# Top-k attention: the guess's last two steps on VectorE, and the softmax division moved from the attention to the projection

## The chip, the cores and the metric

The kernel runs on one core of one Trainium2 chip. The metric is device time in microseconds of one execution. Times are given as the median of several executions; the profile is one further execution taken by the hardware profiler.

## The reference

Two attention layers over x of shape [2, 256, 48, 48], so 2304 positions, 8 heads of 32, all in float32. The change touches only the first one:

```python
scores = einsum('bhnd,bhmd->bhnm', q, k) * DHEAD ** (-0.5)
kth = top_k(scores, 64)[0][..., -1:]
masked = where(scores >= kth, scores, finfo.min)
attn = softmax(masked, axis=-1)
o = einsum('bhnm,bhmd->bhnd', attn, v)      # then back to [B, C, H, W]
o = conv1x1(o, Wo, bo) + x                  # project_out
...                                         # two 1x1 convolutions with batch norms, then the second attention
```

Each row of scores keeps its 64 largest; the softmax runs over these.

## The kernel before

The stages follow one another, with a block of instructions per engine in each: `project_heads` (q, k, v), `attention_top`, `project_out`, `mlp`, then the second layer's projection, full attention and output.

`attention_top` works on tiles of 128 query rows against all 2304 keys, two tiles (u = 0 and 1) making a pair. There are 8 heads of 18 pairs, 144 pairs. Each engine has its instructions in an order written out by hand, and waits on semaphores for the others. For one pair:

- TensorE computes the scores of a tile (L363); ScalarE copies them out of PSUM (`keep_scores`, L446) into one of four buffers.
- VectorE takes the eight largest of each chunk of 36 scores, 64 instructions a tile (`chunk_tops`, L565), then `prepare` (L573 to L576). A tile's completion raises `tops_taken`.
- The 64th largest value is sought near a guess. `guess_place` makes the guess in four dependent ScalarE steps for each tile: a weighted sum of the chunks' first two values (L478, with an accumulator), a count of the candidates above it by Sign (L481, likewise), a linear `factor` from that count (L484), and the product of factor and sum (L487).
- `select` on VectorE waits for both guesses (L590), marks and counts the candidates above (L593), finds the next 24 below in three rounds (L598 to L609) and picks the right one (L613). L617 computes whether a row is in doubt. It runs after the first eight instructions of the next pair's `chunk_tops`.
- TensorE and ScalarE condense the doubts to one number (L390 to L392, L467). `hand_on` on VectorE reads it after twelve more of `chunk_tops`, counts again (L635) and if needed searches again (L648, L650) where there is doubt, and then signals `kth_ready` (L671).
- ScalarE writes a penalty (L462), GpSimd subtracts it from the scores (L547), ScalarE takes the exponentials with their sums in an accumulator (L450).
- TensorE transposes the probabilities (L373), ScalarE copies these out (L457), TensorE multiplies them with v into four quadrants (L382). ScalarE copies the quadrants (`parts`, L531), TensorE adds them (L401), and `finish` (L495) copies the two tiles' results out, each scaled by its row's 1/sum, which `invert_sums` (L676) made on VectorE.

ScalarE's order in one turn of the loop is: guess of tile 0 of the next pair, exponentials of tile 0, scores, guess of tile 1, two copies of transposed blocks, exponentials of tile 1, three copies, scores, the doubt, two copies, the wait for `kth_ready`, the two penalties with three copies between them, `parts`, `finish`.

`project_out` turns the results in 9 chunks of 512 positions (`turn`, L752), ScalarE copies them (L779), TensorE multiplies with the weights (L767), VectorE adds bias and x (L791). TensorE's order is turn(0), then for each chunk c: turn(c + 1), the eight matmuls of chunk c.

Of the kernel before, what the change touches and what calls it, by code (L numbers as in the profile page):

```python
# [19 lines left out]
F32 = mybir.dt.float32  # L20
# [251 lines left out]

def attention_top(nc, cst, operands, q_parts, k_parts, v_all, o_all):

    ctx = ExitStack()
    with ctx:
# [24 lines left out]
        above = sb("above", [P, 1])  # L301
        sums = sb("sums", [P, 2])
        one_by_sum = [sb(f"one_by_sum{n}", [P, 2]) for n in range(2)]
        parts = sb("parts", [P, PAIR])
# [8 lines left out]
        tops_taken, dve_order = sem("tops_taken"), sem("dve_order")  # L313
        guess_steps, guess_ready = sem("guess_steps"), sem("guess_ready")
        doubt_ready, doubt_counted, any_ready = sem("doubt_ready"), sem("doubt_counted"), sem("any_ready")
# [3 lines left out]
        weighed, parts_ready, added, o_kept = sem("weighed"), sem("parts_ready"), sem("added"), sem("o_kept")  # L319
        inverse_ready = sem("inverse_ready")  # L320
        HEAD_PAIRS = B * PAIRS
# [121 lines left out]
        def _(act):  # L443
# [3 lines left out]

            def exponentials(s, tile, parity):
                act.wait_ge(masked_ready, tile + 1)
                act.activation(probs[s % 2][:, :], probs[s % 2][:, :], ACT.Exp, scale=SCALE,  # L450
                               bias=minus_max[parity][:, s % 2:s % 2 + 1], accum_out=sums[:, s % 2:s % 2 + 1]
                               ).then_inc(probs_ready, 1)
# [17 lines left out]
            def guess_place(u, pair, parity):  # L470

                step = (2 * pair + u) * 3
                act.wait_ge(tops_taken, 2 * pair + u + 1)
                act.activation(weighted[:, u, :, :], top8[parity][:, u, 0:CHUNKS, 0:2], ACT.Identity,  # L478
                               scale=-FIRST_GUESS / CHUNKS, accum_out=minus_first[:, u:u + 1]).then_inc(guess_steps, 1)
                act.wait_ge(guess_steps, step + 1)  # L480
                act.activation(compared[:, u, :, :], top8[parity][:, u, 0:CHUNKS, 0:KEEP], ACT.Sign,  # L481
                               bias=minus_first[:, u:u + 1], accum_out=balance[:, u:u + 1]).then_inc(guess_steps, 1)
                act.wait_ge(guess_steps, step + 2)
                act.activation(factor[:, u:u + 1], balance[:, u:u + 1], ACT.Copy, scale=-STEP / 2,  # L484
                               bias=-(1.0 + STEP * (CHUNKS * KEEP / 2 - AIM))).then_inc(guess_steps, 1)
                act.wait_ge(guess_steps, step + 3)
                act.activation(guess[:, u:u + 1], factor[:, u:u + 1], ACT.Identity,  # L487
                               scale=minus_first[:, u:u + 1]).then_inc(guess_ready, 1)

            def finish(s, h, pair, parity):  # L490

                act.wait_ge(inverse_ready, pair + 1)
                act.wait_ge(added, pair + 1)
                for u in range(2):
                    last = act.activation(o_all[:, s + u, cols(h * D, D)], ps_o[:, O_COL + D * u:O_COL + D * u + D],  # L495
                                          ACT.Identity, scale=one_by_sum[parity][:, u:u + 1])
                last.then_inc(o_kept, 1)

# [6 lines left out]
            for u in range(2):  # L505
                penalty(u, 0)
            with act.Fori(0, HEADS) as h:
                for p in range(HEAD_PAIRS):
                    pair, tile, s, parity = h * HEAD_PAIRS + p, h * HEAD_TILES + 2 * p, 2 * p, p % 2
                    guess_place(0, pair + 1, 1 - parity)  # L510
                    exponentials(s, tile, parity)
                    keep_scores(s + 4, tile + 4)
                    guess_place(1, pair + 1, 1 - parity)
                    keep_turned(s, 0, tile)
                    keep_turned(s, 1, tile)
                    exponentials(s + 1, tile + 1, parity)
# [12 lines left out]
                    penalty(1, 1 - parity)  # L529
                    act.wait_ge(weighed, tile + MCH + 3)  # L530
                    act.activation(parts[:, :], ps_o[:, 0:PAIR], ACT.Copy).then_inc(parts_ready, 1)  # L531
                    finish(s, h, pair, parity)

# [17 lines left out]
        def _(dve):  # L551
# [27 lines left out]
            def select(pair, tops):  # L579
# [7 lines left out]
                below_of = lambda u: below[:, u, :].rearrange("p (c k) -> p c k", k=KEEP)  # L587
                marks_of = lambda u: scratch[:, 0:(CHUNKS + REST) * KEEP].rearrange("p (c k) -> p c k", k=KEEP)
                after(at["n"])
                wait_alone(dve, guess_ready, 2 * pair + 2)  # L590
                written = [0, 0]
# [81 lines left out]

            def invert_sums(tile, pair, parity):
                wait_alone(dve, probs_ready, tile + 2)
                dve.reciprocal(one_by_sum[parity][:, :], sums[:, :]).then_inc(inverse_ready, 1)  # L676

            dve.memset(flag[:, :], 0.0)
# [6 lines left out]

            def pair_step(pair, tile, p, before=2):

                def between(c):
                    if c == 7 and before > 0:
                        select(pair - 1, top8[(p - 1) % 2])  # L690
                    if c == 19 and before > 0:
                        hand_on(pair - 1, (p - 1) % 2)
                        if before > 1:
                            invert_sums(tile - 4, pair - 2, p % 2)

                chunk_tops(tile, 2 * p, between)
                chunk_tops(tile + 1, 2 * p + 1)
                prepare(pair, top8[p % 2])

            for p in range(2):  # L700
                pair_step(p, 2 * p, p, before=p)
            with dve.Fori(0, HEADS - 1) as h:
# [5 lines left out]
            dve.wait_ge(doubt_ready, ALL_PAIRS)  # L708
            dve.sem_inc(tops_taken, 2)
            invert_sums(HEADS * HEAD_TILES - 4, ALL_PAIRS - 2, 0)  # L710
            hand_on(ALL_PAIRS - 1, 1)
# [3 lines left out]
            dve.sem_inc(kth_ready, 1)  # L715
            invert_sums(HEADS * HEAD_TILES - 2, ALL_PAIRS - 1, 1)


def project_out(nc, cst, xs, o_all, x, w_o, b_o, mlp_weights, next_sources):

# [3 lines left out]
    with ctx:  # L724
        sb = lambda name, shape, dt=F32: ctx.enter_context(nc.sbuf_tensor("r_" + name, shape, dt))
        sem = lambda name: ctx.enter_context(nc.semaphore("r_" + name))
        w, bias = sb("w", [P, KC, C]), sb("bias", [P, KC])
        a = [sb(f"a{n}", [P, KC, CW]) for n in range(2)]
# [3 lines left out]
        turned, a_ready, proj_done, added = sem("turned"), sem("a_ready"), sem("proj_done"), sem("added")  # L732
        xf = xs[:, :, :, :].rearrange("p k b n -> p k (b n)")
        block = ctx.enter_context(nc.Block())
# [10 lines left out]
        def _(pe):  # L745
            def turn(c):
                for kc in range(KC):
                    n = KC * c + kc
# [32 lines left out]
        @block.vector  # L781
        def _(dve):
            dve.wait_ge(w_loaded, 32)
            for c in range(NCH):
                for piece in first_needed(c):
                    dve.wait_ge(x_loaded[piece], 16 * KC)
                for oc in range(KC):
# [3 lines left out]
                    dve.scalar_tensor_tensor(x_c, ps[n % 4][:, :], bias[:, oc:oc + 1], x_c,  # L791
                                             ALU.add, ALU.add).then_inc(added, 1)


# [515 lines left out]
def build(nc, t, out):  # L1310
# [4 lines left out]
    with ctx:  # L1315
# [4 lines left out]
        with ExitStack() as top:  # L1320
# [7 lines left out]
            o_top = top.enter_context(nc.sbuf_tensor("o_top", [P, B * MCH, C], F32))  # L1328
            attention_top(nc, cst, operands, q_parts, k_parts, v_top, o_top)
            project_out(nc, cst, xs, o_top, t["x"], t["w_o"], t["b_o"], mlp_weights, t)  # L1330
        mlp(nc, cst, xs, x1, mlp_weights, t["w_2"], (t["w_k1"], t["w_q1"], t["w_v1"]))
# [42 lines left out]
```

## Time and profile before

| | us |
|---|---|
| median of 3 executions | 5868.32 (5866.23 to 5868.85) |
| the profiled execution, its time | 5872.33 |
| the profiled execution, its span | 5870.2 |
| busy: TensorE, VectorE, ScalarE, GpSimd | 4366.5, 4365.0, 4327.3, 1500.0 |
| mean granted TensorE clock | 0.819 |

The span is from the first to the last instruction of the core. Busy times are of one profiled execution, and a busy TensorE is not a TensorE at its peak. In the rows, PE is TensorE, DVE VectorE, ACT ScalarE, POOL GpSimd, and L12 is line 12 of the kernel. "Idle before" is the time for which the engine had nothing to do just ahead of an instruction, with the releaser that ended it; "issue" there means that the profile shows none.

### The profile page before, as it was taken

The numbers are of one execution on the slowest core, as the hardware profiler recorded it, in microseconds if no ns is written. First come the engines' busy times: TensorE is split into PE (matmuls) and PEld (weight loads), VectorE is DVE, ScalarE is ACT, GpSimd is POOL, SyncE is SP. The second block draws the span as 40 slices with busy tenths as digits, with TensorE's granted clock in tenths as the row PEclk, the third lists the DMA queues.
The fourth block names the chain that finished last, engine by engine and source line by source line (L and its number), as shares of the span: only waits on it lengthen the run. The fifth ranks groups of instructions, "written<-read, shape, count | busy, mean of one in ns | idle before, by whom it ended". The sixth has DMA issues, their size and how long they took to land. (4 is left out here: it accounts for less than half of the span.)

```text
span 5870.2 us, 115806 instructions
## 1 busy us (share of the span) xinstructions
PE 4366.5 (74%) x32459; PEld 2810.7 (48%) x32459; DVE 4365.0 (74%) x25530; ACT 4327.3 (74%) x6804; POOL 1500.0 (26%) x362
## 2 busy tenths in 40 slices
PE   7565566666676366666666666998999999999998
PEld 4343344444444244444444444435556556655655
DVE  4888888888888888888888887313577777777775
ACT  2787799888898588988899889342567666666765
POOL 0343344443444244434444444001000000000000
PEclk8676677777777677777777777998999999999999
DMA  5000000000000000000000000102210101001012
GB/s 188 6 16 14 6 15 16 7 15 15 7 16 15 4 15 10 12 15 14 8 15 15 7 15 14 41 7 101 93 29 21 29 20 30 20 21 28 22 28 82
DMA packets 79588, 154.72 MB, mean 26 GB/s; under 512 B 8120, under 2 KB 49464, under 8 KB 73528
## 3 DMA queue, kind: packets, MB, share of 16 engines
q1 hardware_dynamic: 78904, 146.72, 8.8%
q8 instruction: 293, 4.80, 0.3%
q14 instruction: 391, 3.20, 0.2%
HBM read 99.50 MB, written 47.19 MB: 25 GB/s over the span
## 5 line engine op out<-in xcount | busy, mean ns | idle before, releaser
L565 DVE MAX8 a_top<-a_scores 128x8 f32<-128x36 f32 x18432 | 1829.3, 180 | 254.9 <-ACT a_scores L446 254.5
L547 POOL TENSOR_TENSOR a_probs<-a_scores,a_probs 128x2304 f32<-128x2304 f32 x288 | 1458.1, 5084 | 2081.7 <-ACT a_probs L462 2081.7
L373 PE MATMUL a_ps_t<-ident,a_probs 128*128 128x128 f32 x5184 | 976.8, 326 | 1045.4 <-ACT a_probs_t L457 685.8
L373 PEld LDWEIGHTS a_ps_t<-ident,a_probs 128*128 128x128 f32 x5184 | 675.4, 164 | 1333.9 <-ACT a_probs_t L457 865.0
L1108 PE MATMUL b_ps_t<-ident,b_soft 128*128 128x128 f32 x5184 | 795.2, 286 | 97.2 <-ACT b_soft_t L1181 68.7
L462 ACT ACTIVATE a_probs<-a_scores,a_steep_kth 128x2304 f32<-128x2304 f32 x290 | 641.1, 2211 | 294.1 <-DVE a_minus_max L671 294.1
L1193 DVE TENSOR_SCALAR_CACHE_REDUCE b_soft<-b_ps_s 128x2304 f32<-128x2304 f32 x290 | 741.6, 2557 | 89.0 <-PE b_ps_s L1095 70.1
L1181 ACT ACTIVATE b_soft_t<-b_ps_t 128x512 f32<-128x512 f32 (+1 forms) x864 | 438.0, 525 | 488.4 <-PE b_ps_t L1108 487.7
L1108 PEld LDWEIGHTS b_ps_t<-ident,b_soft 128*128 128x128 f32 x5184 | 558.6, 142 | 450.2 <-issue 304.1
L457 ACT ACTIVATE a_probs_t<-a_ps_t 128x512 f32<-128x512 f32 (+1 forms) x1440 | 725.7, 546 | 18.2 <-PE a_ps_t L373 6.8
L363 PE MATMUL a_ps_s<-a_k_stack,a_q_ring 128*128 128x512 f32 (+1 forms) x1465 | 652.2, 605 | 13.5 <-ACT a_scores L446 8.9
L1166 ACT ACTIVATE b_soft<-b_soft,b_minus_max 128x2304 f32<-128x2304 f32 x289 | 642.1, 2222 | 13.2 <-DVE b_soft L1193 13.0
L450 ACT ACTIVATE a_probs<-a_probs,a_minus_max 128x2304 f32<-128x2304 f32 x288 | 635.9, 2208 | 1.6 <-POOL a_probs L547 1.6
L1213 DVE COPY b_soft_t<-b_ps_t 128x512 f32<-128x512 f32 x576 | 383.5, 688 | 320.8 <-PE b_ps_t L1108 320.1
L446 ACT ACTIVATE a_scores<-a_ps_s 128x2304 f32<-128x2304 f32 x292 | 606.8, 2078 | 13.3 <-PE a_ps_s L363 13.3
L382 PE MATMUL a_ps_o<-a_probs_t,a_v 128*32 128x128 f32 x10368 | 580.2, 304 | 0.8
L363 PEld LDWEIGHTS a_ps_s<-a_k_stack,a_q_ring 128*128 128x128 f32 x1465 | 436.5, 322 | 156.5 <-ACT a_scores L446 64.0
L1126 PE MATMUL b_ps_o<-b_soft_t,b_v 128*32 128x256 f32 x5184 | 457.6, 395 | 7.6 <-DVE o_all L1201 7.2
L1074 POOL COPY b_v<-v_all 128x576 f32 x16 | 10.6, 668 | 1548.1 <-PE b_ps_o L1126 1439.7
L1095 PE MATMUL b_ps_s<-b_k_stack,b_q_ring 128*128 128x512 f32 (+1 forms) x1450 | 383.2, 395 | 6.5 <-PEq L166 3.3
L382 PEld LDWEIGHTS a_ps_o<-a_probs_t,a_v 128*32 128x32 f32 x10368 | 265.1, 115 | 227.9 <-issue 116.3
L401 PE MATMUL a_ps_o<-add_up,a_parts 128*128 128x32 f32 x576 | 149.0, 398 | 255.8 <-ACT a_parts L531 255.8
(126 smaller groups left out, 4420.7 us busy)
## 6 DMA issues: line engine op xcount, KB each, us to landing
a_k_stack<-k_parts SPq DMA_DIRECT2D x72, 288.0 KB, 5.9
b_k_stack<-k_parts SPq DMA_DIRECT2D x72, 288.0 KB, 6.0
a_q_ring<-q_parts SPq DMA_DIRECT2D x294, 64.0 KB
b_q_ring<-q_parts SPq DMA_DIRECT2D x294, 64.0 KB
k_parts<-p_high SPq DMA_DIRECT2D x36, 256.0 KB, 2.1
k_parts<-p_rest SPq DMA_DIRECT2D x36, 256.0 KB, 2.1
q_parts<-p_high SPq DMA_DIRECT2D x36, 256.0 KB, 2.0
q_parts<-p_rest SPq DMA_DIRECT2D x36, 256.0 KB, 2.0
```

Of the source, the lines that this page charges most:

```text
L363: last = pe.matmul(ps_s[:, c:c + n], q_ring[pair % AHEAD_Q][:, P * (s % 2):P * (s % 2) + P], k_stack[b][:, c:c + n], start=True, stop=True)
L373: last = pe.transpose(ps_t[(NTG * s + g) % 2][:, P * m:P * m + P], probs[s % 2][:, P * (m0 + m):P * (m0 + m) + P], cst["ident"][:, :])
L382: last = pe.matmul(ps_o[rows, P * (s % 2):P * (s % 2) + P], v_s[s // MCH][:, m, :], probs_t[:, m, :], start=m < 4, stop=m + 4 >= MCH)
L446: act.activation(scores_all[:, s % 4, :], ps_s[:, 0:N], ACT.Copy).then_inc(scores_kept, 1)
L450: act.activation(probs[s % 2][:, :], probs[s % 2][:, :], ACT.Exp, scale=SCALE, bias=minus_max[parity][:, s % 2:s % 2 + 1], accum_out=sums[ ...
L457: act.activation(probs_t[:, m0:m0 + n, :], ps_t[(NTG * s + g) % 2][:, 0:n * P].rearrange("p (m q) -> p m q", q=P), ACT.Copy).then_inc(turn ...
L462: act.activation(probs[u][:, :], scores_all[:, 2 * parity + u, :], ACT.Relu, scale=-STEEP, bias=steep_kth[parity][:, u:u + 1]).then_inc(pe ...
L547: pool.tensor_tensor(probs[u][:, :], scores_all[:, 2 * (p % 2) + u, :], probs[u][:, :], ALU.subtract).then_inc(masked_ready, 1)
L565: last = dve.max(top8[s // 2 % 2][:, s % 2, c, :], scores_all[:, s % 4, CHUNK * c:CHUNK * c + CHUNK])
L1108: last = pe.transpose(ps_t[(NTG * s + g) % 2][:, P * m:P * m + P], soft[s % 3][:, P * (m0 + m):P * (m0 + m) + P], cst["ident"][:, :])
L1166: act.activation(soft[s % 3][:, :], soft[s % 3][:, :], ACT.Exp, scale=-1.0, bias=minus_max[s % 3][:, 0:1], accum_out=sums[s % 2][:, 0:1]). ...
L1193: dve.tensor_scalar(soft[s % 3][:, :], ps_s[:, 0:N], -SCALE, None, ALU.mult, ALU.min, accum_out=minus_max[s % 3][:, 0:1]).then_inc(shifted ...
```

## The change

- The guess's steps 3 and 4 (L484, L487) leave ScalarE. `select` on VectorE now waits for the two `balance` values and computes `factor` and `guess` for both tiles with one tensor_scalar and one tensor_tensor of two columns.
- What stays on ScalarE for tile 0 (L478, L481) is issued between the copy of `parts` and `finish`, in the turn of the loop before the one in which it stood.
- `finish` copies both tiles' undivided results in one instruction. `invert_sums` is gone. The sums of all rows and heads are kept in one buffer of 36 x 8 columns, which the exponentials write through their accumulator at a head-dependent address.
- `project_out` begins with a reciprocal of that buffer on VectorE. `divide(c)`, one tensor_tensor of 1024 columns in place, precedes each chunk; TensorE's `turn(c)` waits for it. The first two are issued at the start, `divide(c + 2)` behind the two additions of chunk c.

```diff
@@ ScalarE
-    step = (2 * pair + u) * 3
     act.wait_ge(tops_taken, 2 * pair + u + 1)
     act.activation(weighted[:, u, :, :], top8[parity][:, u, 0:CHUNKS, 0:2], ACT.Identity,
-                   scale=-FIRST_GUESS / CHUNKS, accum_out=minus_first[:, u:u + 1]).then_inc(guess_steps, 1)
-    act.wait_ge(guess_steps, step + 1)
+                   scale=-FIRST_GUESS / CHUNKS, accum_out=minus_first[:, u:u + 1]).then_inc(first_guessed, 1)
+    act.wait_ge(first_guessed, 2 * pair + u + 1)
     act.activation(compared[:, u, :, :], top8[parity][:, u, 0:CHUNKS, 0:KEEP], ACT.Sign,
-                   bias=minus_first[:, u:u + 1], accum_out=balance[:, u:u + 1]).then_inc(guess_steps, 1)
-    act.wait_ge(guess_steps, step + 2)
-    act.activation(factor[:, u:u + 1], balance[:, u:u + 1], ACT.Copy, scale=-STEP / 2,
-                   bias=-(1.0 + STEP * (CHUNKS * KEEP / 2 - AIM))).then_inc(guess_steps, 1)
-    act.wait_ge(guess_steps, step + 3)
-    act.activation(guess[:, u:u + 1], factor[:, u:u + 1], ACT.Identity,
-                   scale=minus_first[:, u:u + 1]).then_inc(guess_ready, 1)
+                   bias=minus_first[:, u:u + 1], accum_out=balance[:, u:u + 1]).then_inc(balance_ready, 1)
...
-def finish(s, h, pair, parity):
-    act.wait_ge(inverse_ready, pair + 1)
+def finish(s, h, pair):
     act.wait_ge(added, pair + 1)
-    for u in range(2):
-        last = act.activation(o_all[:, s + u, cols(h * D, D)], ps_o[:, O_COL + D * u:O_COL + D * u + D],
-                              ACT.Identity, scale=one_by_sum[parity][:, u:u + 1])
-    last.then_inc(o_kept, 1)
+    act.activation(o_all[:, s:s + 2, cols(h * D, D)],
+                   ps_o[:, O_COL:O_COL + 2 * D].rearrange("p (u d) -> p u d", d=D),
+                   ACT.Copy).then_inc(o_kept, 1)
...
+guess_place(0, 1, 1)                     # once, ahead of the loop
 with act.Fori(0, HEADS) as h:
     for p in range(HEAD_PAIRS):
-        guess_place(0, pair + 1, 1 - parity)
-        exponentials(s, tile, parity)
+        exponentials(s, h, tile, parity)
...
         act.activation(parts[:, :], ps_o[:, 0:PAIR], ACT.Copy).then_inc(parts_ready, 1)
-        finish(s, h, pair, parity)
+        guess_place(0, pair + 2, parity)
+        finish(s, h, pair)
@@ VectorE, select
-    wait_alone(dve, guess_ready, 2 * pair + 2)
+    dve.wait_ge(balance_ready, 2 * pair + 2)
+    factors = counted(dve.tensor_scalar(factor[:, :], balance[:, :], -STEP / 2,
+                                        -(1.0 + STEP * (CHUNKS * KEEP / 2 - AIM)), ALU.mult, ALU.add))
+    after(factors)
+    guesses = counted(dve.tensor_tensor(guess[:, :], factor[:, :], minus_first[:, :], ALU.mult))
+    after(guesses)
@@ VectorE
-def invert_sums(tile, pair, parity):
-    wait_alone(dve, probs_ready, tile + 2)
-    dve.reciprocal(one_by_sum[parity][:, :], sums[:, :]).then_inc(inverse_ready, 1)
@@ project_out, TensorE
 def turn(c):
+    pe.wait_ge(divided, c + 1)
@@ project_out, VectorE
+def divide(c):
+    o_c = o_all[:, 4 * c:4 * c + 4, :].rearrange("p m (h d) -> p m h d", d=D)
+    inverse_c = one_by_sum[:, 4 * c:4 * c + 4, :].unsqueeze(3).to_broadcast([P, 4, HEADS, D])
+    dve.tensor_tensor(o_c, o_c, inverse_c, ALU.mult).then_inc(divided, 1)
+
+dve.reciprocal(one_by_sum[:, :, :], sums[:, :, :]).then_inc(inverse_ready, 1)
+dve.wait_ge(inverse_ready, 1)
+divide(0)
+divide(1)
 dve.wait_ge(w_loaded, 32)
 for c in range(NCH):
...
+    if c + 2 < NCH:
+        divide(c + 2)
```

## Rows read from the trace of the kernel before

**Rows 1.** L671's instructions: ns min/median/max, first and last start in us.
```profile
L671 DVE TENSOR_SCALAR a_minus_max<-a_extremes x144: 159/161/165, 141.3 to 3649.7; 128x2 f32<-128x2 f32 x144
```

**Rows 2.** Waits of VectorE and ScalarE, 100 to 3680 us: total, times, longest.
```profile
DVE a_top L565 <- ACT a_scores L446: 254.5, 142, 4.5
...
ACT a_probs L462 <- DVE a_minus_max L671: 294.1, 144, 58.2
```

**Rows 3.** Timeline of one undisturbed pair: start, us, engine, line, instruction [idle before].
```profile
2091.05 10.56 DVE L565 MAX8 a_top<-a_scores 128x8 f32<-128x36 f32 x108
2091.06 2.21 ACT L462 ACTIVATE a_probs<-a_scores,a_steep_kth 128x2304 f32<-128x2304 f32 x1 [0.29 <-DVE a_minus_max L671]
...
2093.35 10.12 POOL L547 TENSOR_TENSOR a_probs<-a_scores,a_probs 128x2304 f32<-128x2304 f32 x2 [12.76 <-ACT a_probs L462]
...
2096.68 0.37 ACT L531 ACTIVATE a_parts<-a_ps_o 128x256 f32<-128x256 f32 x1
...
2097.98 2.27 PE L363 MATMUL a_ps_s<-a_k_stack,a_q_ring 128*128 128x512 f32 x5
2098.36 0.46 ACT L495 ACTIVATE o_top<-a_ps_o,a_one_by_sum 128x32 f32 x2 [1.31 <-PE a_ps_o L401]
2098.71 0.32 ACT L478 ACTIVATE a_weighted<-a_top 128x128 f32<-128x128 f32 x1
...
2099.74 0.20 ACT L484 ACTIVATE a_factor<-a_balance 128x1 f32<-128x1 f32 x1
...
2100.17 2.20 ACT L450 ACTIVATE a_probs<-a_probs,a_minus_max 128x2304 f32<-128x2304 f32 x1
...
2102.32 0.62 DVE L576 TENSOR_REDUCE a_extremes<-a_top 128x4 f32<-128x256 f32 x1
2102.37 2.07 ACT L446 ACTIVATE a_scores<-a_ps_s 128x2304 f32<-128x2304 f32 x1
...
2104.59 0.88 DVE L565 MAX8 a_top<-a_scores 128x8 f32<-128x36 f32 x8 [1.65 <-ACT a_scores L446]
...
2105.13 0.19 ACT L481 ACTIVATION_READ_ACCUMULATOR a_compared<-a_top,a_minus_first 128x1 f32 x1
...
2105.58 0.29 ACT L487 ACTIVATE a_guess<-a_factor,a_minus_first 128x1 f32<-128x1 f32 x1
...
2106.03 0.44 DVE L593 TENSOR_SCALAR_CACHE_REDUCE a_below<-a_top,a_guess 128x216 f32<-128x216 f32 x1 [0.57 <-issue]
...
2113.70 2.22 ACT L462 ACTIVATE a_probs<-a_scores,a_steep_kth 128x2304 f32<-128x2304 f32 x1 [0.27 <-DVE a_minus_max L671]
```

**Rows 4.** Timeline: the start of L462 in a pair with a recount.
```profile
2068.16 2.21 ACT L462 ACTIVATE a_probs<-a_scores,a_steep_kth 128x2304 f32<-128x2304 f32 x1 [8.50 <-DVE a_minus_max L671]
```

**Rows 5.** L595's instructions, ns min/median/max.
```profile
L595 DVE TENSOR_TENSOR a_beyond<-a_extremes,a_top x144: 153/156/163, 134.5 to 3643.0; 128x2 f32<-128x2 f32 x144
```

**Rows 6.** Timeline of the first projection, TensorE and VectorE.
```profile
3681.57 1.94 PE L752 MATMUL r_ps_t<-ident,o_top 128*128 128x128 f32 x8 [0.32 <-PEq L276]
...
3685.71 1.97 PE L752 MATMUL r_ps_t<-ident,o_top 128*128 128x128 f32 x8 [2.19 <-DMA r_bias<-b_o]
...
3700.07 1.04 PE L752 MATMUL r_ps_t<-ident,o_top 128*128 128x128 f32 x8
3700.28 0.75 DVE L791 SCALAR_TENSOR_TENSOR xs<-r_ps,r_bias,xs 128x512 f32<-128x512 f32 x1 [0.96 <-PE r_ps L767]
3700.95 3.60 PE L767 MATMUL r_ps<-r_a,r_w 128*128 128x512 f32 x8
```

**Rows 7.** VectorE's groups by form: busy us, mean ns, idle before.
```profile
L1003 DVE TENSOR_TENSOR m_hid<-m_hid,xs 128x1024 f32<-128x1024 f32 x9 | 11.0, 1226 | 9.6 <-ACT m_hid L942 9.6
...
L1008 DVE RECIPROCAL m_norm<-m_norm 128x36 f32<-128x36 f32 x1 | 0.4, 377 | 0.0
```

**Rows 8.** Timeline of TensorE, second layer's start, and the last projection.
```profile
4043.37 1.93 PE L903 MATMUL m_ps_h<-m_hid,ones 128*128 128x512 f32 x2 [1.19 <-POOL m_hid L958]
...
5838.37 3.67 PE L1283 MATMUL o_ps<-o_a,o_w 128*128 128x512 f32 x8 [1.84 <-DVE o_y L1306]
```

More of the change, by code:

```diff
@@ L270, in _, with attention_top @@
                     dve.tensor_copy(v_all[:, n, :], ps_v[n % 2][:, :]).then_inc(v_kept, 1)
-def attention_top(nc, cst, operands, q_parts, k_parts, v_all, o_all):
+def attention_top(nc, cst, operands, q_parts, k_parts, v_all, o_all, sums):
     ctx = ExitStack()
@@ L301, in attention_top @@
         above = sb("above", [P, 1])
-        sums = sb("sums", [P, 2])
-        one_by_sum = [sb(f"one_by_sum{n}", [P, 2]) for n in range(2)]
         parts = sb("parts", [P, PAIR])
@@ L313, in attention_top @@
         tops_taken, dve_order = sem("tops_taken"), sem("dve_order")
-        guess_steps, guess_ready = sem("guess_steps"), sem("guess_ready")
+        first_guessed, balance_ready = sem("first_guessed"), sem("balance_ready")
         doubt_ready, doubt_counted, any_ready = sem("doubt_ready"), sem("doubt_counted"), sem("any_ready")
@@ L319, in attention_top @@
         weighed, parts_ready, added, o_kept = sem("weighed"), sem("parts_ready"), sem("added"), sem("o_kept")
-        inverse_ready = sem("inverse_ready")
         HEAD_PAIRS = B * PAIRS
@@ L446, in keep_scores, with exponentials @@
                 act.activation(scores_all[:, s % 4, :], ps_s[:, 0:N], ACT.Copy).then_inc(scores_kept, 1)
-            def exponentials(s, tile, parity):
+            def exponentials(s, h, tile, parity):
                 act.wait_ge(masked_ready, tile + 1)
                 act.activation(probs[s % 2][:, :], probs[s % 2][:, :], ACT.Exp, scale=SCALE,
-                               bias=minus_max[parity][:, s % 2:s % 2 + 1], accum_out=sums[:, s % 2:s % 2 + 1]
+                               bias=minus_max[parity][:, s % 2:s % 2 + 1], accum_out=sums[:, s, cols(h, 1)]
                                ).then_inc(probs_ready, 1)
@@ L515, in _ @@
                     keep_turned(s, 1, tile)
-                    exponentials(s + 1, tile + 1, parity)
+                    exponentials(s + 1, h, tile + 1, parity)
                     keep_turned(s, 2, tile)
@@ L587, in select @@
                 below_of = lambda u: below[:, u, :].rearrange("p (c k) -> p c k", k=KEEP)
-                marks_of = lambda u: scratch[:, 0:(CHUNKS + REST) * KEEP].rearrange("p (c k) -> p c k", k=KEEP)
                 after(at["n"])
-                wait_alone(dve, guess_ready, 2 * pair + 2)
+                dve.wait_ge(balance_ready, 2 * pair + 2)
[4 more added lines that the diff above has]
+                after(guesses)
                 written = [0, 0]
@@ L684, in _, with pair_step @@
             dve.wait_ge(buffers_set, 1)
-            def pair_step(pair, tile, p, before=2):
+            def pair_step(pair, tile, p, before=True):
                 def between(c):
-                    if c == 7 and before > 0:
+                    if c == 7 and before:
                         select(pair - 1, top8[(p - 1) % 2])
-                    if c == 19 and before > 0:
+                    if c == 19 and before:
                         hand_on(pair - 1, (p - 1) % 2)
-                        if before > 1:
-                            invert_sums(tile - 4, pair - 2, p % 2)
                 chunk_tops(tile, 2 * p, between)
@@ L700, in _ @@
             for p in range(2):
-                pair_step(p, 2 * p, p, before=p)
+                pair_step(p, 2 * p, p, before=p > 0)
             with dve.Fori(0, HEADS - 1) as h:
@@ L708, in _ @@
             dve.wait_ge(doubt_ready, ALL_PAIRS)
-            dve.sem_inc(tops_taken, 2)
-            invert_sums(HEADS * HEAD_TILES - 4, ALL_PAIRS - 2, 0)
+            dve.sem_inc(tops_taken, 3)
             hand_on(ALL_PAIRS - 1, 1)
@@ L715, in _, with project_out @@
             dve.sem_inc(kth_ready, 1)
-            invert_sums(HEADS * HEAD_TILES - 2, ALL_PAIRS - 1, 1)
-def project_out(nc, cst, xs, o_all, x, w_o, b_o, mlp_weights, next_sources):
+def project_out(nc, cst, xs, o_all, sums, x, w_o, b_o, mlp_weights, next_sources):
     CW = BANK
@@ L727, in project_out @@
         w, bias = sb("w", [P, KC, C]), sb("bias", [P, KC])
+        one_by_sum = sb("one_by_sum", [P, B * MCH, HEADS])
         a = [sb(f"a{n}", [P, KC, CW]) for n in range(2)]
@@ L732, in project_out @@
         turned, a_ready, proj_done, added = sem("turned"), sem("a_ready"), sem("proj_done"), sem("added")
+        inverse_ready, divided = sem("inverse_ready"), sem("divided")
         xf = xs[:, :, :, :].rearrange("p k b n -> p k (b n)")
@@ L1328, in build @@
             o_top = top.enter_context(nc.sbuf_tensor("o_top", [P, B * MCH, C], F32))
-            attention_top(nc, cst, operands, q_parts, k_parts, v_top, o_top)
-            project_out(nc, cst, xs, o_top, t["x"], t["w_o"], t["b_o"], mlp_weights, t)
+            sums = top.enter_context(nc.sbuf_tensor("sums_top", [P, B * MCH, HEADS], F32))
+            attention_top(nc, cst, operands, q_parts, k_parts, v_top, o_top, sums)
+            project_out(nc, cst, xs, o_top, sums, t["x"], t["w_o"], t["b_o"], mlp_weights, t)
         mlp(nc, cst, xs, x1, mlp_weights, t["w_2"], (t["w_k1"], t["w_q1"], t["w_v1"]))
```

## The prediction, made before the change ran

> **What bounds the kernel now.** I read the page first. The four engines share the work so evenly that no busy share decides anything. The first attention takes most of the span, and nearly all of the change lies in it, so I went there. L671, which signals `kth_ready`, runs once for each pair of tiles, 144 times between 141.3 and 3649.7, so one pair of tiles takes 3508.4 / 143 = 24.53 us on average [rows 1].
>
> Next the waits. In every pair ScalarE waits for VectorE (L462 for L671), VectorE waits for ScalarE (L565 for L446), and ScalarE waits 1.3 us for TensorE (L495 for L401) [rows 2, 3]. Engines that wait for each other in turn mean that a loop through them sets the pace, so I followed one undisturbed pair in the timeline [rows 3]. Call the start of its first L462 T (2091.06); the next such start is 2113.70, so the period is 22.64 us. The loop is this:
>
> - T to 2096.68: ScalarE empties `ps_t`, writes the penalties, then copies `parts`.
> - 2096.68 to 2098.36: TensorE adds the quadrants; ScalarE has nothing to do for 1.31 us of it.
> - 2098.36 to 2100.17: the two L495, then the whole of the guess for tile 0.
> - 2100.17 to 2104.44: the exponential and L446, which hands VectorE new scores.
> - 2104.59: VectorE, idle for 1.65 us, starts eight L565. At 2106.03 L593 starts; from there it is 7.67 us to the next L462, which has itself waited 0.27 us.
>
> VectorE's own work is no limit before that: L576 ends at 2102.94, the idle 1.65 us follow. Nor is L593's "issue" idle of 0.57 us what it is called: L487 ends at 2105.87 and L593 starts 0.16 us on, about the 0.15 us that L446's end (2104.44) takes to reach L565 (2104.59). L593 waits for ScalarE's guess.
>
> The other 1.9 us of the mean are recounts, in pairs where the guess was doubted: ScalarE waits 8.50 us instead of 0.27 [rows 4], and 294.1 - 144 x 0.27 = 255 us in all [rows 2]. They lie between L617 and L671 and the change leaves them. In such a pair, too, L462 is followed by the same loop, so every interval profits alike.
>
> **The change part by part.** Terms of one interval, T to next T:
>
> First, `finish`. Its two L495 take 0.35 us from first start to the next instruction (2098.36 to 2098.71). One Copy of 64 columns takes their place. L531, a Copy of 256 columns from PSUM, takes 0.37, L446 with 2304 takes 2.07: 0.00083 us a column, so 64 columns take 0.21, and since ScalarE's next instruction starts about 0.10 before the end of such a copy (the two L495 end at 2098.82, L478 starts at 2098.71), 0.11 us to the next start. Saved 0.24; bounds 0.00 (the one copy costs as much as both) and 0.24.
>
> Second, the guess for tile 0. Its first two steps (L478, L481 and their accumulator reads) run from 2098.71 to 2099.74, 1.03 us. They move ahead of `finish`, behind the copy of `parts`, where ScalarE idles 1.31 us waiting for TensorE. So they are hidden; if that cover went they would cost 1.03. They wait for VectorE to have finished the first tile's L565. Of the 108 that start at 2091.05, 44 belong to it: 44 x 10.56 / 108 = 4.3 us, done at 2095.4, 1.3 us ahead of the copy. Saved 1.03. The last two steps (L484, L487) go from 2099.74 to 2100.17. Saved 0.43. Together the exponential could start 1.70 us earlier, at T + 7.41. Two things could be late next. GpSimd's first mask starts at T + 2.29 and two take 10.12, so one ends at T + 7.35: just in time. TensorE's scores for L446 end at 2100.25, T + 9.19, against L446 at T + 9.61: in time. VectorE's own part ends at T + 11.88, minus the reciprocal's slot, against scores at T + 11.83. So this term is 1.70, with 1.46 as the lower bound, and all three neighbours stand close behind it.
>
> Third, guess tile 1 and the two new VectorE steps. Today L593 starts 1.59 us after L446 ends. After, `balance` is there when L481's accumulator read ends (2105.13 + 0.19 = 2105.32) plus 0.16, 2105.48, as the eight L565 end (2105.47). Then a tensor_scalar and a tensor_tensor of 2 columns, each waiting for the one before. L595, the same sort, takes 0.156 [rows 5]; with 0.04 for the dependence each costs 0.20, together 0.40: L593 at 2105.88, 0.15 us earlier than now. VectorE has three waits here and neither row shows what they cost it when none has to be waited out. Bounds: 0.15 gained, 0.20 lost (the 0.57 idle kept whole less ScalarE's 0.43, and a little). I take 0.05 gained, nearer to the rows, which show no gap between dependent steps elsewhere. ScalarE's own 0.43 for tile 1 comes after L446 and shortens only its slack: it then waits for `kth_ready` some 0.6 us instead of 0.27.
>
> The Trainium skill, "VectorE: DVE Perf Modes", section on the TRN2 errata, gives an SBUF to SBUF operation 58 cycles plus its elements over 0.96 GHz, some 62 ns for 2 columns by that estimate; two steps would be 0.12 instead of 0.40 and the total 40 us lower. L595's 156 ns disagrees, and the trace decides.
>
> Fourth, `invert_sums` goes: 0.17 us of VectorE and a wait on `probs_ready`, in its slack, worth nothing; without it VectorE would be the late one after L576. The sums go to a larger buffer at an address that depends on the head; L495 already writes so. Nothing.
>
> One interval gains 1.70 + 0.05 = 1.75 us (1.26 to 1.85), 143 of them 250.3. Before the first T both guesses lose their last steps and gain the VectorE ones: 2 x 0.43 - 0.40 = 0.4. After the last T ScalarE alone leads: 1.70 + 0.43 + about 0.2 for `finish` = 2.3.
>
> **The projection pays.** There TensorE is never idle: 4.31 us a chunk, from turn (1.04) and eight matmuls (3.60) that overlap a little [rows 6]. `turn(c)` now waits for `divide(c)`, and VectorE issues `divide(c + 2)` only after both additions of chunk c, so after that chunk's last matmul. TensorE's next instruction is `turn(c + 2)`. It starts now at 3700.07; after, it starts when the addition (3700.28, 0.75 long, next start 0.08 before its end) and the division are done, and 0.15 for the signal. The division is a tensor_tensor of 1024 columns; L1003 takes 1.23 [rows 7]. 3700.28 + 0.67 + 1.23 + 0.15 = 3702.33, so 2.26 us of idle TensorE, for c from 0 to 6: 7 x 2.26 = 15.8. At the stage's start a reciprocal of 288 columns: 36 take 0.377 [rows 7], and with L595's 0.156 for 2 that is 0.0065 a column, so 2.0 us, then 1.23 for `divide(0)`. From about 3681.4, just before TensorE's first turn, that is 3684.6; turn(0) starts at 3684.75 rather than 3681.57 and ends 1.94 later, 3686.7, when turn(1) starts, now at 3685.71 after a DMA. So 1.0 late. Together 17, lower bound 15.
>
> The upper bound is the clock. This stage runs at full clock now; its first turn after the DMA wait took 1.97 instead of 1.04. With 2.26 us idle in each 6.6 it may fall. L903 shows a low clock behind smaller gaps: 1.93 us for two matmuls of 512 columns after 1.19 idle, where L767 needs 0.90 for two. The last projection shows a high one behind 1.84 (3.67 us for eight) [rows 8]. I take the latter row, the same work. If all seven chunks ran at half clock, each 4.3 longer: 47 in all. The Trainium skill, "TensorE: Matmul & The Clock Gate", "What's actually happening", says that the clock is halved after idling and restored after sustained work; it doesn't decide this case, and both rows fit it.
>
> **The sum.** The profiled execution took 5872.3 (span 5870.2 and 2.1 around it), 4.0 over the median of the three. 5872.3 - 250.3 - 0.4 - 2.3 + 17 = 5636.3; less 4.0: 5632.
>
> **Rivals.** Where a time is given it is against the median.
>
> *Less gained per pair.* The one copy, the waits ahead of the two VectorE steps, or GpSimd's mask, cost what the bounds allow: 1.26 us, 180 in all, 5868.3 - 180 - 3 + 17 = 5702. For it: three neighbours within 0.1 to 0.4 us of the new schedule. Against: dependent steps show no gaps. Something between, 5660 to 5705: 0.20.
>
> *The projection at the lower clock.* Half of the bound 30: 5647, all of it 5662. For it L903, against it the last projection: 0.13.
>
> *VectorE is the bound already and nothing comes of it.* 5868 + 17 - 3 = 5882 if not a microsecond of the loop went; partly so, within 0.2%. Against: its 1.65 idle us in each pair. 0.02.
>
> *Slower: more recounts.* The guess is now multiplied on VectorE. If it came out otherwise, more rows would fall outside the window of 24 and `hand_on` would recount: 8.50 - 0.27 = 8.2 us each. It decides from 236 / 8.2 = 29 more recounts; with 40, 5632 + 328 = 5960. Against: the same formula in the same type. 0.03.
>
> *The forecast*, 5600 to 5660: 0.62.
>
> **Numbers.** The range that leaves out no more than 2 in 10 is 5600 to 5700: its low end is 1.85 a pair and 15 for the projection (5868.3 - 264.6 - 2.7 + 15 = 5616) with a little for the waits that may go with L676, its high end nearly the first rival's. What a measurement here can tell is about 0.2%, 12 us. Faster 0.95, same 0.02, slower 0.03.
>
> **What would show it.** The interval of an undisturbed pair near 20.9; L565 idle before new scores near 0 (now 1.65); L450 at T + 7.4; the evicting copy still waiting, some 0.4 us, for L401; ScalarE waiting about 0.6 for L671; in the projection chunks 6.6 us apart with TensorE waiting 2.3 for the division. An interval over 21.4, with L450 waiting for GpSimd or L593 late by issue, would be the first rival; more recounts than before, and so more than 294 us of ScalarE waiting for L671, the last.

## The result and the profile after

The changed kernel takes 5586.25 us (median, 5584.55 to 5596.08) against 5867.59 us in the same comparison: a ratio of 0.9524, 95% interval 0.9508 to 0.9541. It is 281 us faster where 236 were forecast, and the time lies below the stated range of 5600 to 5700. Busy time hardly tells this: ScalarE has lost 163 us, VectorE has gained 42.

The page of the changed kernel, its busy time per engine:

```profile
span 5582.5 us, 114219 instructions
...
PE 4367.2 (78%) x32459; PEld 2805.0 (50%) x32459; DVE 4406.7 (79%) x25684; ACT 4164.0 (75%) x6084; POOL 1502.2 (27%) x362
```

The intervals, from the instruction that signals `kth_ready` (now L667, to be set beside [rows 1]):

```profile
L667 DVE TENSOR_SCALAR a_minus_max<-a_extremes x144: 159/162/166, 139.2 to 3348.1; 128x2 f32<-128x2 f32 x144
```

143 intervals now take 3208.9 us, 22.44 each, against 3508.4 and 24.53. That is 299.5 us, 2.09 an interval; 1.75 was forecast. The span's other parts: 2.1 us less ahead of the first L667, 16.4 more from the last L667 to the first matmul of the batch-normed stage (the tail of the attention and the projection), 2.5 less behind it. 299.5 + 2.1 - 16.4 + 2.5 = 287.7, the difference of the two spans.

The waits of the changed kernel from 100 to 3500 us (total, times, longest), beside [rows 2]:

```profile
ACT a_probs L462 <- DVE a_minus_max L667: 294.7, 144, 58.2
...
DVE a_steep_kth L666 <- issue: 110.6, 141, 2.9
...
ACT o_top L486 <- PE a_ps_o L401: 50.1, 137, 0.4
...
DVE a_top L557 <- ACT a_scores L446: 45.7, 135, 3.2
...
ACT a_any_doubt L467 <- PE a_ps_o L392: 6.2, 1, 6.2
```

VectorE no longer waits for scores to speak of (46 us, was 255), and ScalarE waits 0.37 us for TensorE's sums instead of 1.31, as forecast. ScalarE's wait for L667 has changed by 0.6 us in all, and the recount's first instruction (L631, now L627) runs 19 times in both kernels, so there were no more recounts. L666 is the row that the prediction had not looked at. Its "issue" idle is 110.6 us; before the change L670's was 154.0.

Now the same pair of the loop as in [rows 3], the 78th, in the changed kernel:

```profile
1928.72 2.22 ACT L462 ACTIVATE a_probs<-a_scores,a_steep_kth 128x2304 f32<-128x2304 f32 x1 [0.30 <-DVE a_minus_max L667]
...
1931.01 10.14 POOL L539 TENSOR_TENSOR a_probs<-a_scores,a_probs 128x2304 f32<-128x2304 f32 x2 [10.47 <-ACT a_probs L462]
...
1934.33 0.37 ACT L522 ACTIVATE a_parts<-a_ps_o 128x256 f32<-128x256 f32 x1
...
1935.95 0.22 ACT L486 ACTIVATE o_top<-a_ps_o 128x64 f32 x1 [0.37 <-PE a_ps_o L401]
1936.22 2.21 ACT L450 ACTIVATE a_probs<-a_probs,a_minus_max 128x2304 f32<-128x2304 f32 x1
...
1938.43 2.07 ACT L446 ACTIVATE a_scores<-a_ps_s 128x2304 f32<-128x2304 f32 x1
...
1940.64 0.88 DVE L557 MAX8 a_top<-a_scores 128x8 f32<-128x36 f32 x8 [0.17 <-ACT a_scores L446]
...
1941.49 0.17 DVE L582 TENSOR_SCALAR a_factor<-a_balance 128x2 f32<-128x2 f32 x1
1941.69 0.16 DVE L585 TENSOR_TENSOR a_guess<-a_factor,a_minus_first 128x2 f32<-128x2 f32 x1
1941.88 0.44 DVE L589 TENSOR_SCALAR_CACHE_REDUCE a_below<-a_top,a_guess 128x216 f32<-128x216 f32 x1
1942.24 2.21 ACT L450 ACTIVATE a_probs<-a_probs,a_minus_max 128x2304 f32<-128x2304 f32 x1
...
1945.84 2.09 ACT L446 ACTIVATE a_scores<-a_ps_s 128x2304 f32<-128x2304 f32 x1
...
1947.07 0.16 DVE L613 SCALAR_TENSOR_TENSOR a_doubt<-a_beyond,a_kth 128x2 f32<-128x2 f32 x1
...
1947.34 0.24 PE L392 MATMUL a_ps_o<-a_doubt,ones 128*1 128x1 f32 x4
...
1947.81 0.14 ACT L467 ACTIVATE a_any_doubt<-a_ps_o 1x3 f32<-1x3 f32 x1
...
1948.94 0.17 DVE L666 TENSOR_SCALAR a_steep_kth<-a_kth 128x2 f32<-128x2 f32 x1 [0.54 <-issue]
...
1949.22 2.22 ACT L462 ACTIVATE a_probs<-a_scores,a_steep_kth 128x2304 f32<-128x2304 f32 x1 [0.29 <-DVE a_minus_max L667]
```

And the end of the same pair in the kernel before, rows that were not read for the prediction:

```profile
2106.74 2.21 ACT L450 ACTIVATE a_probs<-a_probs,a_minus_max 128x2304 f32<-128x2304 f32 x1
...
2110.34 2.09 ACT L446 ACTIVATE a_scores<-a_ps_s 128x2304 f32<-128x2304 f32 x1
...
2111.48 0.24 PE L392 MATMUL a_ps_o<-a_doubt,ones 128*1 128x1 f32 x4
...
2112.31 0.14 ACT L467 ACTIVATE a_any_doubt<-a_ps_o 1x3 f32<-1x3 f32 x1
...
2113.42 0.17 DVE L670 TENSOR_SCALAR a_steep_kth<-a_kth 128x2 f32<-128x2 f32 x1 [0.87 <-issue]
```

Count from T, the start of the first L462, in both:

| | before | after | less |
|---|---|---|---|
| first L450 | 9.11 | 7.50 | 1.61 |
| the guess is applied (L593, L589) | 14.97 | 13.16 | 1.81 |
| the doubt reaches ScalarE (L467) | 21.25 | 19.09 | 2.16 |
| L670, L666 | 22.36 | 20.22 | 2.14 |
| next L462 | 22.64 | 20.50 | 2.14 |

Up to L593 the recorded working holds in the main: 1.81 us came of its parts where 1.75 were forecast, though 0.20 of it comes between the scores and L593, for which 0.05 was taken and 0.15 was the bound. The stretch behind L593, 7.67 us, was taken as VectorE's own and so as fixed; it is 7.34 now. The 0.33 us went out of the idle ahead of L670 (0.87, now 0.54), and L670 stayed 1.11 to 1.13 us behind L467 in this pair.

So the reading is: the interval is not closed by VectorE's chain but by ScalarE's order. The second L446 must end before ScalarE gets to L467, VectorE must have L467's number before it issues L670, and ScalarE has less to do ahead of L467. From the first L446 to the second L450 it takes 3.81 us (1938.43 to 1942.24) where it took 4.37 (2102.37 in [rows 3] to 2106.74). These 0.56 us are tile 1's last two steps (0.43) and 0.13 for which ScalarE waited for L481's number ahead of them. The other side of L467 does not hold it up: in the whole attention it waits for TensorE's count of the doubts (L392) only once, ahead of the first pair. In this pair the count ends 0.59 us before L467 starts in the kernel before and 0.23 in the changed one, so VectorE's `select` is not the bound, but it is no longer far from it.

A third neighbour is nearer still. The first exponential of the changed kernel, L450, waits for GpSimd's first mask (L539), which ends at 1931.01 + 5.07 = 1936.08; L450 starts 0.14 us later, and 0.27 behind `finish` (L486). Five pairs on, `finish` comes later than the mask's end (2041.83 + 5.07 = 2046.90), and L450 follows it after 0.12:

```profile
2041.83 10.15 POOL L539 TENSOR_TENSOR a_probs<-a_scores,a_probs 128x2304 f32<-128x2304 f32 x2 [18.37 <-ACT a_probs L462]
...
2047.02 0.22 ACT L486 ACTIVATE o_top<-a_ps_o 128x64 f32 x1 [0.37 <-PE a_ps_o L401]
2047.14 2.21 ACT L450 ACTIVATE a_probs<-a_probs,a_minus_max 128x2304 f32<-128x2304 f32 x1
```

Over the whole trace L450 starts 0.13 us behind the mask's end in 113 of 143 pairs, however early `finish` was, and 0.12 behind a late `finish` in 23. So in most pairs of the changed kernel a still shorter `finish` should give nothing; no run tried it.

The projection of the changed kernel, TensorE only, beside [rows 6]:

```profile
3381.11 3.31 PE L743 MATMUL r_ps_t<-ident,o_top 128*128 128x128 f32 x16 [3.59 <-DVE o_top L777]
3384.26 3.60 PE L758 MATMUL r_ps<-r_a,r_w 128*128 128x512 f32 x8
3389.84 1.16 PE L743 MATMUL r_ps_t<-ident,o_top 128*128 128x128 f32 x8 [1.98 <-DVE o_top L777]
3390.79 5.28 PE L758 MATMUL r_ps<-r_a,r_w 128*128 128x512 f32 x8
3398.04 1.09 PE L743 MATMUL r_ps_t<-ident,o_top 128*128 128x128 f32 x8 [1.98 <-DVE o_top L777]
...
3404.54 1.09 PE L743 MATMUL r_ps_t<-ident,o_top 128*128 128x128 f32 x8 [1.98 <-DVE o_top L777]
...
3411.05 1.85 PE L743 MATMUL r_ps_t<-ident,o_top 128*128 128x128 f32 x8 [1.98 <-DVE o_top L777]
3412.70 4.56 PE L758 MATMUL r_ps<-r_a,r_w 128*128 128x512 f32 x8
```

TensorE waits 1.98 us for the division ahead of each of seven chunks, which are 6.50 us apart instead of 4.31. Two of the seven ran at the lower clock for a while: the eight matmuls took 5.28 us in one (mean granted clock 0.68 of full), the turn and the matmuls 1.85 and 4.56 in the other (0.54 and 0.80), where 1.09 and 3.60 are usual (1.00).

### The profile page after: what moved, and what is told of

Same layout as the page of the kernel before. It is cut to its first block and busy times, and to the rows that moved or that the text cites. A ratio compares the mean times of both kernels' runs of the same rounds, so it can differ in the third digit from the quotient of the medians.

```text
span 5582.5 us, 114219 instructions
## 1 busy us (share of the span) xinstructions
PE 4367.2 (78%) x32459; PEld 2805.0 (50%) x32459; DVE 4406.7 (79%) x25684; ACT 4164.0 (75%) x6084; POOL 1502.2 (27%) x362
## 5 line engine op out<-in xcount | busy, mean ns | idle before, releaser
L539 POOL TENSOR_TENSOR a_probs<-a_scores,a_probs 128x2304 f32<-128x2304 f32 x288 | 1460.3, 5090 | 1778.2 <-ACT a_probs L462 1778.2
L462 ACT ACTIVATE a_probs<-a_scores,a_steep_kth 128x2304 f32<-128x2304 f32 x290 | 641.2, 2211 | 294.7 <-DVE a_minus_max L667 294.7
L450 ACT ACTIVATE a_probs<-a_probs,a_minus_max 128x2304 f32<-128x2304 f32 x288 | 638.1, 2216 | 28.3 <-issue 17.9
L446 ACT ACTIVATE a_scores<-a_ps_s 128x2304 f32<-128x2304 f32 x292 | 607.0, 2079 | 12.3 <-PE a_ps_s L363 12.3
L401 PE MATMUL a_ps_o<-add_up,a_parts 128*128 128x32 f32 x576 | 149.3, 399 | 257.7 <-ACT a_parts L522 257.7
```

The costliest lines, as they stand in the source:

```text
L446: act.activation(scores_all[:, s % 4, :], ps_s[:, 0:N], ACT.Copy).then_inc(scores_kept, 1)
L462: act.activation(probs[u][:, :], scores_all[:, 2 * parity + u, :], ACT.Relu, scale=-STEEP, bias=steep_kth[parity][:, u:u + 1]).then_inc(pe ...
L539: pool.tensor_tensor(probs[u][:, :], scores_all[:, 2 * (p % 2) + u, :], probs[u][:, :], ALU.subtract).then_inc(masked_ready, 1)
```

## The experiments

The question behind the miss: does the interval run through ScalarE's order up to L467 (the reading above), or through VectorE's own work behind L593 (as recorded), with some other reason for the 0.33 us? And do the parts of the change give what they were each said to give? In the expectations the line numbers of ScalarE and VectorE are those of the kernel that is edited.

### The last two steps alone

```diff
 def guess_place(u, pair, parity):        # ScalarE; stays where it was, ahead of exponentials
...
-    act.activation(factor[:, u:u + 1], balance[:, u:u + 1], ACT.Copy, ...)
-    act.activation(guess[:, u:u + 1], factor[:, u:u + 1], ACT.Identity, ...)
 def select(pair, tops):                  # VectorE
+    factors = counted(dve.tensor_scalar(factor[:, :], balance[:, :], ...))
+    guesses = counted(dve.tensor_tensor(guess[:, :], factor[:, :], minus_first[:, :], ALU.mult))
```

> The kernel before with one edit: the guess's last two steps for both tiles on VectorE. The loop through ScalarE (the interval ends 1.4 us after L467, and L467 is issued when ScalarE gets to it): ScalarE loses 0.43 us ahead of the first L446 and some 0.55 ahead of L467, so 0.98 us an interval, 143 x 0.98 = 140, about 5728 us. The recorded chain (7.67 us of VectorE's own from L593 to the next L462): only 0.43 + 0.15 = 0.58 an interval, 83 us, about 5785. If the two steps on VectorE simply added their 0.40 us to it, 0.03 an interval, about 5864.

Measured 5725.36 us (5724.70 to 5732.94), ratio 0.9758 (0.9741 to 0.9774): 144 us against the kernel before of this comparison (5869.18). Its signalling instruction:

```profile
L669 DVE TENSOR_SCALAR a_minus_max<-a_extremes x144: 159/163/165, 139.0 to 3504.5; 128x2 f32<-128x2 f32 x144
```

3365.5 / 143 = 23.53, so 1.00 an interval: the 0.98 of the loop through ScalarE. The recorded chain would have given 0.58. Tile 1's steps count, though they lie behind the first L446:

```profile
2024.40 2.07 ACT L446 ACTIVATE a_scores<-a_ps_s 128x2304 f32<-128x2304 f32 x1
...
2028.21 2.22 ACT L450 ACTIVATE a_probs<-a_probs,a_minus_max 128x2304 f32<-128x2304 f32 x1
```

That is 3.81 us instead of 4.37, so 0.56, and tile 0 gives 0.56 too, from `finish` to the first L450 (2020.95 to 2022.20, 1.25; it was 2098.36 to 2100.17, 1.81). Together 1.12, by which an undisturbed interval is indeed shorter (21.52, was 22.64). The mean shows 1.00: ScalarE waits 0.08 us more for transposed blocks ahead of the second L446, and nine more pairs have the longer way from L467 to VectorE that is told of at the end. With tile 0's 0.56 and the 0.17 by which the guess comes sooner after the scores here (1.42 us behind L446's end, was 1.59), the recorded chain would still give no more than 0.73. VectorE's two new instructions cost nothing that can be seen.

### The order alone

```diff
+guess_place(0, 1, 1)                     # ahead of the loop
 for p in range(HEAD_PAIRS):
-    guess_place(0, pair + 1, 1 - parity)
...
     act.activation(parts[:, :], ps_o[:, 0:PAIR], ACT.Copy).then_inc(parts_ready, 1)
+    guess_place(0, pair + 2, parity)     # all four steps
     finish(s, h, pair, parity)
```

> The kernel before with one edit: all four guess steps of tile 0 issued between the copy of parts and finish. Both theories: 1.46 us go into the 1.31 us for which ScalarE waits for TensorE, finish starts 0.05 later, so 1.41 an interval, 202 us, about 5666. If it were VectorE's own work that set the interval: no change, 5868.

Measured 5674.72 us (5672.75 to 5679.56), ratio 0.9668 (0.9652 to 0.9684), 194 us. This is the largest part of the change, and it removes no instruction. A chain on VectorE alone is excluded. In the trace L495 follows L487 with no wait:

```profile
2036.80 0.29 ACT L487 ACTIVATE a_guess<-a_factor,a_minus_first 128x1 f32<-128x1 f32 x1
2037.01 0.45 ACT L495 ACTIVATE o_top<-a_ps_o,a_one_by_sum 128x32 f32 x2
```

### The division alone

```diff
-last = act.activation(o_all[:, s + u, ...], ps_o[...], ACT.Identity, scale=one_by_sum[parity][:, u:u + 1])
+act.activation(o_all[:, s:s + 2, ...], ps_o[...], ACT.Copy)          # one for both tiles
-invert_sums(...)                                                     # and all of project_out as changed
```

> The kernel before with one edit: undivided results copied in one piece and the division in the projection. Recorded: 0.24 an interval saved (34 us), 17 lost in the projection, about 5851. By the trace of the changed kernel, in which L450 starts 0.27 after the one copy instead of 0.35 after the first of two: 0.08 an interval (11 us) saved, 18 lost, about 5875.

Measured 5852.74 us (5847.94 to 5858.41), ratio 0.9970 (0.9958 to 0.9983). The recorded term was right, the second guess wrong: L668 runs from 143.2 to 3615.8, so 24.28 us an interval and 0.25 saved. The trace shows why:

```profile
2059.42 0.22 ACT L493 ACTIVATE o_top<-a_ps_o 128x64 f32 x1 [1.25 <-PE a_ps_o L401]
2059.54 0.32 ACT L478 ACTIVATE a_weighted<-a_top 128x128 f32<-128x128 f32 x1
```

The next instruction starts 0.12 us after the one copy, for which 0.11 was forecast. In the full change the next is L450, which waits for GpSimd's mask and starts 0.27 after, as shown above.

### Fewer VectorE instructions ahead of L670, in the kernel before

```diff
-if c == 19 and before > 0:
+if c == 16 and before > 0:
     hand_on(pair - 1, (p - 1) % 2)
```

> The kernel before with one edit: hand_on after 17 of the next tile's maxima instead of 20, so three L565 (0.29 us) fewer ahead of L670. The loop through ScalarE: L670 still starts 1.1 us after L467, no change, 5868 within 0.2%. The recorded chain: 0.29 an interval less, 42 us, about 5826.

Measured 5874.36 us (5867.52 to 5876.83), ratio 1.0007 (0.9997 to 1.0017): no change. VectorE's waits in this run:

```profile
DVE a_steep_kth L670 <- issue: 103.8, 67, 2.8
DVE a_steep_kth L670 <- ACT a_any_doubt L467: 90.3, 77, 1.6
```

The three maxima now run behind `hand_on`, and in their old place stands idle: 194.1 us ahead of L670 where there were 155.6 (154.0 and 1.6), 0.27 more each time. And now that the wait is longer, the profile names what it is for in 77 of the cases: L467. It had called the same wait "issue".

### The same edit in the changed kernel

```diff
-if c == 19 and before:
+if c == 16 and before:
     hand_on(pair - 1, (p - 1) % 2)
```

> The changed kernel with hand_on three L557 earlier. If L467 on ScalarE still sets L666 (1.13 us behind it in both kernels): no change, 5586 within 0.2%, and some 0.27 us more idle ahead of L666. If after the change VectorE's own work has become the bound: 0.29 an interval, 41 us, about 5545.

Measured 5589.27 us (5588.80 to 5589.51), 0.9521 (0.9506 to 0.9537) against the kernel before; the changed kernel's own ratio is 0.9524. No change:

```profile
DVE a_steep_kth L666 <- issue: 135.9, 131, 2.8
...
DVE a_steep_kth L666 <- ACT a_any_doubt L467: 14.5, 13, 1.7
```

150.4 us of idle in place of 114.3, so 0.25 more each time. VectorE's maxima ahead of L666 do not set the interval after the change either. The edit says nothing of `select`, which runs before them; for that there is L467, which in this run too waits for TensorE's count only once.

### One more instruction on ScalarE, in the changed kernel

```diff
 keep_scores(s + 5, tile + 5)
+act.activation(spare[:, :], cst["ones"][:, :], ACT.Copy)
 keep_any(pair + 1)
```

> The changed kernel with one more copy of 128 columns on ScalarE (about 0.2 us to the next start) just ahead of L467. The loop through ScalarE's L467: 0.2 an interval, some 29 us, about 5615. If ScalarE's place in the loop ended at L446, as recorded in the prediction, the 0.3 to 0.6 us for which it waits for L667 would cover it: no change, 5586.

Measured 5614.07 us (5612.57 to 5619.78), ratio 0.9567 (0.9551 to 0.9583): 28 us over the changed kernel. The instruction ahead of L669 runs from 140.2 to 3378.0, 22.64 an interval, 0.20 more. The added copy takes just that long in ScalarE's order:

```profile
1942.66 0.31 ACT L513 ACTIVATE a_spare<-ones 128x128 f32<-128x128 f32 x1
1942.86 0.15 ACT L468 ACTIVATE a_any_doubt<-a_ps_o 1x3 f32<-1x3 f32 x1
```

All of it arrives in the interval, though ScalarE idles 0.3 us ahead of L462 a little later. That idle is no slack: it is the way of the signal from ScalarE to VectorE and back.

### The division ahead of the additions, in the changed kernel

```diff
 for c in range(NCH):
+    if c + 2 < NCH:
+        divide(c + 2)
     for piece in first_needed(c):
...
-    if c + 2 < NCH:
-        divide(c + 2)
```

> The changed kernel with divide(c + 2) issued ahead of the additions of chunk c. If the 1.98 us of TensorE's waiting in each of seven chunks come from that order: 13.9 us, and 2 to 3 more from chunks at the lower clock behind them, about 5570. If the division's own time or its access pattern held TensorE up: no change.

Measured 5571.62 us (5569.69 to 5573.47), ratio 0.9491 (0.9475 to 0.9507), 15 us under the changed kernel and the fastest of all. TensorE in its projection:

```profile
3382.03 3.31 PE L743 MATMUL r_ps_t<-ident,o_top 128*128 128x128 f32 x16 [3.59 <-DVE o_top L777]
...
3388.60 1.04 PE L743 MATMUL r_ps_t<-ident,o_top 128*128 128x128 f32 x8
3389.48 3.60 PE L758 MATMUL r_ps<-r_a,r_w 128*128 128x512 f32 x8
3392.91 1.04 PE L743 MATMUL r_ps_t<-ident,o_top 128*128 128x128 f32 x8
```

The chunks are 4.31 us apart again, all at the full clock, with the same division in the same pattern. Only the start of the stage still pays, one wait of 3.59 us ahead of the first turn. By the traces, from the last signal of the attention to the first matmul of the next stage, it saved 18.7 us (93.6, now 74.9). In this run the start of the attention came 1.6 us later and the stages behind took 5.2 us longer than in the changed kernel's trace; over all the traces of this case these two vary by 4 and by 6 us.

## Why the prediction missed

The sign was right, and so was the kind of mechanism: a loop through the engines, shortened on ScalarE. The path that the loop takes behind L593 was wrong, and by it one term was too small, which put the time out of the range.

- **The step that failed** is the third part of the sum, "ScalarE's own 0.43 for tile 1 comes after L446 and shortens only its slack", with the 7.67 us from L593 to the next L462 taken as fixed. The loop goes on along ScalarE's order to L467. The term of 0.05 an interval measured 0.56 in the order of ScalarE where the guess's steps were moved alone, and 0.53 in the whole change: the table's 2.14 less 1.61. The sixth experiment shows the same from the other side: 0.20 us put ahead of L467 lengthen the interval by 0.20. Over 143 intervals the mean was 2.09 against 1.75, which is 49 us, more than the whole miss. The range shared the error: its best case of 1.85 an interval kept the 7.67 too.
- **Why it was misread.** The idle ahead of L593 was taken apart (a wait for L487 called "issue"), while the same label ahead of L670 was passed over. The doubt has to be waited for and read there, and L467 stood in the timeline 1.11 us ahead.
- **The first part, `finish`:** 0.24 forecast, 0.25 measured by itself. In the whole change it gave about 0.08 (0.35 less 0.27), for L450 then waits for GpSimd's mask. The prediction called that mask "just in time" at T + 7.35, and left out the 0.13 us from its end to L450. That is the neighbour of the first rival that did bind, for some 0.15 us an interval.
- **The order:** 1.03 us of two steps hidden behind the 1.31; all four moved alone gave 3508.4 - 3313.0 = 195.4 us, 1.37 an interval. In the changed kernel 0.37 of the wait is left, 0.4 was forecast. L450 stands at T + 7.50, for which 7.4 was said.
- **The two VectorE steps:** 0.20 each from start to start (1941.49, 1941.69, 1941.88), as priced. The Trainium skill, "VectorE: DVE Perf Modes", in its section on the TRN2 errata, gives about 62 ns for such an operation by its cycle formula, an estimate; L582 lasts 0.17 and L585 0.16 us here, so the trace stands against it. The same section says that this formula falls short of single operations, and its other one for an fp32 tensor_tensor, (N + 151) / 0.96, gives 159 ns as an estimate for two columns, with which the trace agrees. The two steps are off the path all the same, for what VectorE loses there it takes out of its wait for L467.
- **The parts do not add:** 1.00, 1.37 and 0.25 make 2.62, the whole 2.09. It is clearer in undisturbed intervals (22.64 before; 21.52, 21.23 and 22.34 in the first three experiments, 20.50 in the whole): 1.12, 1.41 and 0.30 make 2.83, the whole 2.14, so 0.69 less. Tile 0's last two steps with the wait ahead of them (0.56) are saved once by leaving ScalarE and once by being hidden behind TensorE, and the way from `finish` to L450 is 0.15 longer than behind the one copy in the third experiment. That makes 0.71.
- **The projection:** 17 less the tail's 2.3, so 14.7, against 16.4. The division was priced at 1.23 and takes 1.22, the reciprocal at 2.0 and takes 1.95. The seven chunks cost 2.19 each instead of 2.26, and two drops of the clock cost 1.7 each, for which a rival stood. The stage's first matmul with the weights came 0.6 late instead of 1.0, and the eight that it begins took 3.60 where they had taken 4.15, which gives that back; so the near agreement of the sum is in part luck.
- **The rivals:** less gained per pair did not come, though GpSimd's mask took its 0.15; VectorE as the bound is excluded by the fourth and fifth experiments for its maxima ahead of `kth_ready`, and for `select` by L467, which does not wait for what `select` leads to; the recounts did not grow. The lower clock came in two chunks of seven.
- **Signs that were named:** right were VectorE's idle before new scores, 0.17 (near 0), and L401's wait, 0.37; near were the chunks of the projection, 6.50 us apart with 1.98 of waiting (6.6 and 2.3). The undisturbed interval was to be near 20.9 and is 20.50. One was wrong: ScalarE's wait for L667 stayed 0.29 in this pair where 0.6 was said. A wait that does not grow when its engine gets faster was the mark of a loop through that engine.

What stays open: in both kernels the intervals at some fixed places of the 18-pair loop are about 0.33 us longer than the others, 22.97 against 22.64 before and 20.82 against 20.50 after. The traces show where: from L467's start to L670's (L666's) it takes 1.10 to 1.15 us in 82 of the 144 pairs and 1.40 to 1.50 in 44, the same pairs in both kernels; one more takes 1.8, and 17 have a recount, over 9 us. ScalarE's order up to L467 has the same length in both sorts. So 0.10 us of the 1.9 an interval that the prediction gave to recounts is this. Why VectorE takes longer there, no experiment asked. It cancels between the two kernels; in the first experiment 53 pairs are of the longer sort and in the third 51, which is 0.02 us an interval.

## What to carry to other kernels

Follow the loop until it closes: from a start on one engine to the next start of the same instruction, naming a releaser for each gap. A gap called "issue" ahead of an instruction that depends on another engine's result, a register read behind a semaphore among them, is to be treated as a wait until the distance to that result says otherwise. Take the distance in many turns, not in one. To test whether an engine's own work is the bound, move a few of its instructions out of the stretch and see whether they return as idle time.

When work is handed from an engine's critical order to another engine in a later stage, look at what it stands behind there. The same nine divisions cost 18.7 us more behind the additions than ahead of them, by the traces.

## What the runs showed of the hardware

- A small copy on ScalarE between two others costs its duration less 0.1 to 0.11 us: one copy of 64 columns from PSUM lasts 0.22 and delays the next by 0.12, one of 128 columns from SBUF lasts 0.31 and delays it by 0.20.
- From ScalarE's L467 to VectorE's next instruction, which depends on a register loaded from what L467 wrote, it takes 1.10 to 1.15 us in 82 pairs and 1.40 to 1.50 in 44, in both kernels, and it stays so when three maxima between them go elsewhere.
- From the end of GpSimd's mask to the exponential that waits for it on ScalarE it takes 0.13 us, in 113 of the changed kernel's pairs.
- TensorE's granted clock fell in two of seven chunks, each with 1.98 us of idling ahead, and stayed at its 2.4 GHz level in the other five with the same idling. In the third experiment it fell in one of the seven. Without the idling, in the last experiment, all stayed at the 2.4 GHz level. The Trainium skill, "TensorE: Matmul & The Clock Gate", section "What's actually happening", tells of the two levels, half after idling and full after sustained work; the trace agrees with the levels and shows no fixed rule from one such gap.
